# Weight loads one per batch, the table cleared at the start, turned maxima copied by ScalarE, and a new order for the end of the kernel

## What is computed

```python
# x: 16 batches x 128 rows x 512; ctx has the same shape; 8 heads, 8 experts
x = x + tanh(g_xattn) * xattn(layernorm(x), ctx, ctx)
x = x + tanh(g_ffn) * ffn(layernorm(x), wg, W, b)

# xattn: per head softmax(q^T k / 4) over 512 keys, times v
# ffn: a switch layer. each of the 2048 rows goes to one expert
idx  = argmax(softmax(xt @ wg))
gate = softmax(xt @ wg)[idx]
out  = gate * (W[idx] @ xt + b[idx])
```

## Time and profile before

| | us |
|---|---|
| median of three runs | 562.26 |
| the three runs | 562.48, 562.26, 553.67 |
| the profiled execution | 557.37 |
| its span, first to last instruction | 555.6 |
| busy in the span: PE / DVE / ACT / POOL | 498.3 / 436.1 / 349.5 / 343.9 |

### The profile page before, as it was taken

One profiled execution on the slowest core, in us unless ns is written; L12 is line 12 of the kernel. 1 busy time (PEld: TensorE's weight loads), 2 busy tenths in 40 slices (PEclk: granted clock), 3 DMA queues, 4 the chain that ended last, 5 costly groups with the idle time before them and its releaser, 6 DMA issues.

```text
span 555.6 us, 10053 instructions
## 1 busy us (share of the span) xinstructions
PE 498.3 (90%) x2539; PEld 177.6 (32%) x2580; DVE 436.1 (78%) x851; ACT 349.5 (63%) x428; POOL 343.9 (62%) x531
## 2 busy tenths in 40 slices
PE   0389999899999999999999999978899879899993
PEld 0012223232333333233333333322233134345441
DVE  5898989798898999989999989949788768334341
ACT  3226877778888888888887887945768831111110
POOL 7544476667676767777676787854275445645541
PEclk9999999999999999999999999979999999999998
DMA  4873546665565747565565847564669944643410
GB/s 137 240 160 119 145 119 202 176 181 171 159 168 163 199 126 228 162 182 166 163 196 127 235 130 199 184 162 102 175 187 309 334 176 159 208 148 107 126 59 0
DMA packets 51760, 92.96 MB, mean 167 GB/s; under 512 B 22898, under 2 KB 24946, under 8 KB 51688
## 3 DMA queue, kind: packets, MB, share of 16 engines
q1 hardware_dynamic: 36624, 67.33, 42.6%
q0 software_dynamic: 10560, 24.93, 13.9%
q10 hardware_dynamic: 4536, 0.23, 0.6%
HBM read 68.96 MB, written 28.41 MB: 175 GB/s over the span
## 4 chain that ended last, share of the span: by engine, by line
PE 62%; DVE 15%; DMA 10%; issue 4%; SPq 2%; ACT 2%; POOL 2%; ACTq 2%; POOLq 0%; DVEq 0%; another core or an unknown queue 0%
PE ps_pv L1382 17%; PE ps_ring L1340 17%; PE ps_scores L1359 14%; PE ps_scores L1443 10%; DVE neg_max L951 4%; DVE neg_max L1196 3%; DMA sums<-high_num 2%; DMA slot_tokens<-table_dram,slot_block 2%; DMA stacks<-shift_parts 2%; ACTq L842 2%; DMA sums<-low_num 1%; PE ps_scores L1426 1%; PE ps_ring L1345 1%; PE ps_ring L1402 1%; DMA recs<-recs_dram,token_cols 1%
## 5 line engine op out<-in xcount | busy, mean ns | idle before, releaser
L951 DVE TENSOR_REDUCE neg_max<-ps_ring 128x1 f32<-128x512 f32 x480 | 306.9, 681 | 29.0 <-PE ps_ring L1340 28.2
L852 ACT ACTIVATE probs<-ps_scores 128x1024 f32<-128x1024 f32 x256 | 251.6, 1023 | 65.9 <-PE ps_scores L1359 59.8
L1340 PE MATMUL ps_ring<-stacks 96*128 96x512 bf16 x480 | 166.9, 386 | 7.9 <-DVE neg_max L951 6.4
L1359 PE MATMUL ps_scores<-stacks 128*128 128x512 bf16 x471 | 145.4, 384 | 8.3 <-DMA stacks<-shift_parts 3.5
L1382 PE MATMUL ps_pv<-probs,v_ones 128*32 128x512 f32 x992 | 133.0, 608 | 0.1
L1340 PEld LDWEIGHTS ps_ring<-stacks 96*128 96x128 bf16 x480 | 46.6, 97 | 158.4 <-DVE neg_max L951 113.1
L1443 PE MATMUL ps_scores<-w_sb,f_xt 128*128 x184 | 83.5, 595 | 1.2 <-issue 1.2
L1359 PEld LDWEIGHTS ps_scores<-stacks 128*128 128x128 bf16 x512 | 48.2, 100 | 58.7 <-ACT probs L852 15.0
L828 ACT COPY f_xt<-ps_scores 128x512 f32<-128x512 f32 x22 | 12.9, 586 | 74.0 <-PE ps_scores L1426 74.0
L680 POOL DMA_INDIRECT recs<-recs_dram,token_cols x23 | 23.7, 1029 | 33.3 <-DVE y_outs L1164 16.0
L1443 PEld LDWEIGHTS ps_scores<-w_sb,f_xt 128*128 128x128 f32 x184 | 33.1, 190 | 34.6 <-issue 34.6
(11 more groups left out here) (144 smaller groups left out, 492.9 us busy)
## 6 DMA issues: line engine op xcount, KB each, us to landing
stacks<-parts_dram SPq DMA_DIRECT2D x224, 64.0 KB, 3.1
parts_dram<-prep POOLq DMA_DIRECT2D x15, 768.0 KB, 4.7
recs_dram<-rec SPq DMA_DIRECT2D x16, 512.0 KB, 3.7
w_sb<-w_t SPq DMA_DIRECT2D x16, 512.0 KB, 6.9
stacks<-parts_dram SPq DMA_DIRECT2D x32, 192.0 KB, 3.3
prep<-x_perm SPq DMA_DIRECT2D x16, 256.0 KB, 2.7
prep<-k_perm SPq DMA_DIRECT2D x16, 256.0 KB, 3.0
v_in<-v_t SPq DMA_DIRECT2D x16, 256.0 KB, 2.8
```

Source lines behind the costliest of these rows:

```text
L852: nc.scalar.activation(probs[:, k % 2, 2 * jp:2 * jp + 2], ps_scores[:, jp], ACT.Exp).then_inc(exp_done, 1)
L951: nc.vector.tensor_reduce(neg_max[:, g, j, c:c + 1], ps_ring[:, SLOT[tile]], AX.X, ALU.max, negate=True).then_inc(ring_free, 1)
L1340: nc.tensor.matmul(ps_ring[:, SLOT[tile]], q_stack[0:KS, into.p, g, j, c * 128:(c + 1) * 128], k_stack[0:KS, into.p, g, j], start=True, st ...
L1359: last = nc.tensor.matmul(ps_scores[:, jp, j % 2], k_stack[0:KA, B.p, g, j, c * 128:(c + 1) * 128], q_stack[0:KA, B.p, g, j], start=True, ...
```

## The change

The weights are loaded one piece per batch: piece 0 before batch 0, piece B in batch B, between the store and the spread of the high reciprocals. The table is cleared before batch 0. The two turned maxima of a batch get semaphores of their own (`turned_full`, `turned_taken`), so the ring counts 32 entries, and ScalarE copies them: the high half after the exponentials of step 0 and before `read_high`, the next batch's low half after those of step 4 and before `read_low`. Only the very first copy stays with VectorE.

At the end, `turn_slot(0)` moves behind the last values, and the routing of batch 14 behind it; only slot 0 is turned before the first expert, every next slot is turned in the middle of an expert. VectorE turns the last sums when the values are done, without waiting for ScalarE's read, and ScalarE's read waits for the turning. VectorE's `name_experts(1)`, `take_tiles(1)` and `take_columns(1)` come later, slot 0's bias earlier, and the counting of tiles of the last phase moves behind slot 2's combine. GpSimd reads the table for the second phase after the last norm's scale, and scatters before it waits for new columns.

```diff
-RING_FIRST, RING_BATCH = 1, 34
+RING_BATCH = 32
...
-NUMBER = {name: n for n, name in enumerate(e for e in ENTRIES if e not in ("rows", "route"))}
+NUMBER = {name: n for n, name in enumerate(e for e in ENTRIES if e[0] == "t" and e[:4] != "turn")}
...
+def turned(B, g):
+    return B.b * 2 + (g + 1)
...
+        turned_full, turned_taken = sem("turned_full"), sem("turned_taken")
...
+            def load_weight(B):
 
                 n = NC * NE * DM // NB
-                for piece in range(first, first + pieces):
-                    sp.dma_start(w_sb[:].rearrange("p c e n -> p (c e n)")[:, piece * n:(piece + 1) * n], w_t[piece]
-                                 ).then_inc(w_loaded, 16)
+                sp.dma_start(w_sb[:].rearrange("p c e n -> p (c e n)")[:, bass.ds(B.b * n, n)],
+                             w_t[bass.ds(B.b, 1)].rearrange("o p n -> (o p) n")).then_inc(w_loaded, 16)
+
+            def clear_table():
+
+                sp.wait_ge(pool_const, POOL_CONSTS)
+                sp.dma_start(table_dram.rearrange("(k h p) o -> k h (p o)", h=WIDE // 2, p=256 // WIDE),
+                             none_i[:].unsqueeze(1).to_broadcast([128, WIDE // 2, 256])).then_inc(table_set, 16)
...
+            clear_table()
+            load_weight(Batch(0, 0))
...
                 if prev and by_transfer(B.plus(-1)):
                     store_recips(B.plus(-1), 1)
+                    load_weight(B)
                     spread_recips(B.plus(-1), 1)
+                elif B.known(NB - 1):
+                    load_weight(B)
                 if prev and nxt:
                     load_values(B.plus(1))
-                if B.known(NB - 4):
-                    load_weights(0, 2)
-                if B.known(NB - 3):
-                    load_weights(2, 2)
-                if B.known(NB - 2):
-                    load_weights(6, 4)
-                if B.known(NB - 1):
-                    load_weights(10, 6)
...
-                if B.known(NB - 3):
-                    load_weights(4, 2)
...
-                if B.known(1):
-                    sp.wait_ge(pool_const, POOL_CONSTS)
-                    sp.dma_start(table_dram.rearrange("(k h p) o -> k h (p o)", h=WIDE // 2, p=256 // WIDE),
-                                 none_i[:].unsqueeze(1).to_broadcast([128, WIDE // 2, 256])).then_inc(table_set, 16)
...
-                if g == 1:
-                    pool.wait_ge(ring_free, ring_base(B) + (1 if B.known(NB - 1) else NUMBER["turn1"] + 1))
-                else:
-                    pool.wait_ge(ring_free, RING_FIRST if B.known(0) else ring_base(B.plus(-1)) + (NUMBER["turn0"] + 1))
+                pool.wait_ge(turned_taken, turned(B, g))
...
-                read_slots(1)
...
             rstd2(last)
+            read_slots(1)
             for s in range(NSLOT):
+                first = s + NREC in (PHASES[1][1], FIRST_LATE)
                 if s == 2:
                     number_places(3)
                     store_tokens(*GROUPS[3])
+                if first:
+                    scatter(s)
...
-                    wait(pool, y_ready, s + 1)
                     gather(s + NREC)
+                if not first:
+                    scatter(s)
                 if s == 2:
                     read_slots(2)
-                scatter(s)
...
+                if B.known(NB - 1):
+                    act.wait_ge(high_turned, NB - TURNED)
...
+            def take_maxima(B, g):
+
+                act.wait_ge(turned_full, turned(B, g))
+                stand_alone(act)
+                wait(act, shift_in[g], B.b * 48)
+                if not isinstance(B.b, int):
+                    stand_alone(act)
+                nc.scalar.copy(shift[:, g], ps_ring[0:NJ * NC, SLOT[("turn0", "turn1")[g]], 0:128]).then_inc(turned_taken, 1)
...
+                    if k == 0:
+                        take_maxima(B, 1)
                     if k == 0 and prev:
                         read_high(B.plus(-1))
+                    if k == NC and nxt:
+                        take_maxima(B.plus(1), 0)
...
+                if s == 2:
+                    norm2(Batch(7, 1))
                 if s == 3:
-                    norm2(Batch(7, 1))
                     take_rows(Batch(7, 1))
-                if s == 4:
                     exp_gates(3)
                 evacuate(s, turned_bank(s))
...
-            def take_maxima(B, entry, g, slot):
-
-                dve.wait_ge(ring_full, entry)
-                wait(dve, shift_in[g], B.b * 48)
-                nc.vector.tensor_copy(shift[:, g], ps_ring[0:NJ * NC, slot, 0:128]).then_inc(ring_free, 1)
+            def take_first_maxima():
+
+                dve.wait_ge(turned_full, 1)
+                nc.vector.tensor_copy(shift[:, 0], ps_ring[0:NJ * NC, 0, 0:128]).then_inc(turned_taken, 1)
...
-                dve.wait_ge((low_read, high_read)[g], B.b + 1)
+                if B.known(NB - 1) and g == 1:
+                    dve.wait_ge(pv_done, NB * STEPS)
+                else:
+                    dve.wait_ge((low_read, high_read)[g], B.b + 1)
...
-                take_maxima(B, ring_base(B) + 1, 1, SLOT["turn1"])
...
-                name_experts(1)
-                take_tiles(1)
...
-                        if at == (0, 2):
-                            take_maxima(B, base + (NUMBER["turn1"] + 1), 1, SLOT["turn1"])
-                        if at == (NC, 2):
-                            take_maxima(B.plus(1), base + (NUMBER["turn0"] + 1), 0, SLOT["turn0"])
...
             turn_sums(last, 1)
             invert_sums(last, 1)
+            add_bias(0)
+            take_logits(last.plus(-1))
             turn_back(last)
             add_attention(last)
-            take_logits(last.plus(-1))
-            take_columns(1)
-            add_bias(0)
             for s in range(NSLOT):
                 if s == 2:
                     take_logits(last)
                     find_experts(3)
                     find_gates(3)
+                    take_columns(1)
                     take_ranks(3, ps_ring[:, 0, RANK_AT:])
                     find_places(3)
+                    add_bias(2)
+                if s == 3:
                     count_tiles(2)
                     find_blocks(2)
-                if s == 3:
                     name_experts(2)
                 if s == 4:
                     take_columns(2)
                 combine(s, ps_y[:, s % 2])
-                if s + 1 < NSLOT:
+                if s + 1 < NSLOT and s != 1:
                     add_bias(s + 1)
+                if s == 0:
+                    name_experts(1)
+                    take_tiles(1)
...
+                elif held == "turn1":
+                    wait(pe, turned_taken, turned(B.plus(-1) if ago else B, 1))
+                elif held == "turn0":
+                    wait(pe, turned_taken, turned(B if ago else B.plus(1), 0))
...
-                    if k == 7 and B.known(NB - 1):
-                        pe.wait_ge(ranks_taken, 3)
-                        turn_slot(0, turned_bank(0))
...
+            pe.wait_ge(ranks_taken, 3)
+            turn_slot(0, turned_bank(0))
+            route(last.plus(-1))
             pe.wait_ge(w_loaded, 16 * NB)
-            turn_slot(1, turned_bank(1))
 
             def turn_next(s):
 
-                wait(pe, f_xt_ready, s)
-                turn_slot(s + 1, turned_bank(s + 1))
+                if s + 1 < NSLOT:
+                    wait(pe, f_xt_ready, s)
+                    turn_slot(s + 1, turned_bank(s + 1))
+
+            def rank_and_turn(s):
+                rank(3, ps_ring[:, 0, RANK_AT:])
+                turn_next(s)
 
             for s in range(NSLOT):
                 if s == 1:
-                    route(last.plus(-1))
-                if 0 < s and s + 1 < NSLOT and s + 1 != FIRST_LATE:
-                    turn_next(s)
-                if s == 2:
+                    expert(s, {2: lambda: turn_next(1), 3: lambda: turn_rows(last)})
+                elif s == 2:
                     route(last)
-                if s == 1:
-                    expert(s, lambda: turn_rows(last), 3)
-                elif s == 2:
-                    expert(s, lambda: rank(3, ps_ring[:, 0, RANK_AT:]))
-                elif s + 1 == FIRST_LATE:
-                    expert(s, lambda: turn_next(FIRST_LATE - 1))
+                    expert(s, {2: lambda: rank_and_turn(2)})
                 else:
-                    expert(s)
+                    expert(s, {2: lambda: turn_next(s)})
```

19 lines of the change are left out of this document (9 added, 10 removed).

## The result

| | before | after |
|---|---|---|
| median, 20 runs each | 559.56 | 549.87 |
| lowest to highest | 553.67 to 564.23 | 545.32 to 555.34 |
| ratio after to before | | 0.9827, interval 0.9803 to 0.9852 |
| profiled execution, its span | 557.37, 555.6 | 547.24, 545.6 |

The change gains 1.7%, about 9.7 us. The forecast of 540 had a gain of 19.7 by its sum, so half of it is missing.

What follows compares the result with a forecast made beforehand. The prediction took TensorE to set the pace in the middle; its terms summed to a gain of 19.7, giving 537.7 from the profiled 557.37 or 542.6 from the median 562.26; it said 540, range 531 to 550.

Steps and rivals of the forecast that it cites:

- rival 1: Tail gives nothing because another late gather replaces the one removed; gain 12.9, time 547; chance 0.14.
- Rival 2: Stalls of batches 12 to 14 come from stack loads and the store, half of 10.1 stays; 545; chance 0.09.
- What bounds the kernel: In the middle TensorE sets the pace; VectorE and ScalarE cost time only where TensorE waits for them.
- Table clearing: Moving it from the end of batch 1 to the start gains 2.8 in batch 2 and costs 0.5 at the start.
- three pieces in a row at the quickest landing, less some 7: Upper bound on the start's loss: 9.6 less some 7 between SP's issue and ScalarE's cast for batch 3, 2.6.
- ScalarE idle for parts in batch 0 for more than 1 us: Sign, at the start of the loop, that would show the forecast wrong.
- Weights: One piece per batch gains 5.2, 4.3 and 0.6 in batches 12, 13 and 14, and costs 0 in the loop.
- Rival 3: Weights delay the spread by 1.0 us in each of 13 batches, giving back 13; 553; chance 0.11.
- Rival 4: Weight piece ahead of the spreads in SP's queue delays them, deciding at 5.4 landing; up to 574, slower; chance 0.04.
- Maxima by ScalarE: Copies moved from VectorE gain 0.5 in batches 9 to 11, 13 and 14, price 0 in the body.
- Batch 15 to the first expert: Turning of slot 0 0.6, shorter shift-row wait 0.7, copy wait -0.3, earlier first expert 1.8; gain 2.8.
- The first eight slots: TensorE's work of 33.4 less 0.95, plus 1.5 idle, makes 34.0 of 38.04; gain 4.0.

Runs made afterwards that it cites:

- u_double: Changed kernel, table clearing and first weight piece issued after batch 2's parts landed, plus a second, unread 512 KB piece in batches 1 to 13; 553.62 us.
- u_endw: Changed kernel, but weights loaded as before in batches 12 to 15, none in the loop; 558.51 us, ratio 0.9965 to the kernel before.
- b_weights: Kernel before, with only the weights loaded one piece per batch, the first once the parts of batch 2 had landed; 548.51 us, ratio 0.9803.
- u_read: Changed kernel, but GpSimd issues the third table read ahead of the scatter of slot 2; 545.18 us, ratio 0.9776 to the kernel before.
- u_turn: Changed kernel, but the record of slot 7 is turned behind the whole of expert 6, not in its middle; 548.45 us, ratio 0.9791.
- after_again: The changed kernel itself, unedited, run once more beside other variants on one chip; 549.20 us, ratio 0.9824 to the kernel before.
- u_onehot: Changed kernel, but in batch 13 VectorE finds experts five maxima later and ScalarE takes their exponentials one step later; 546.57 us, ratio 0.9760.
- x_plain: Changed kernel with weights loaded late as before, VectorE copying the maxima, and the table cleared once batch 2's parts had landed; 554.18 us, ratio 0.9896.
- u_clear: Changed kernel, but table clearing and first weight piece are issued only when the parts of batch 2 have landed; 545.61 us, ratio 0.9781.
- u_vcopy: Changed kernel, but VectorE copies the turned maxima as before, with the new semaphores kept; 548.47 us, ratio 0.9818 to the kernel before.
- the three best versions: Changed kernel with later clearing, one-hot, slot 7 turning and first bias, and earlier third table read; 539.79 and 541.90 us, or 539.56 with VectorE copying maxima.

## Why the prediction was wrong, step by step

The forecast added up to 19.7, and the parts below to 8.5 in means of the stretches. The largest pieces of the difference are 3.8 in the tail (5.8 forecast, 2.0 measured), 3.0 at the start (a loss of 0.5 forecast, 3.5 measured) and 2.6 in batches 12 to 14. That the time, 549.87, still lies just under the upper end of the range, 550, was luck: that end was set for rivals 1 and 2, and the loss at the start is in neither.

**What bounds the kernel.** Right. TensorE's busy time did not move, and every gain and loss is one of its waits, but for what the lower clock costs in the tail.

**Table clearing.** The gain in batch 2 was right (2.8 forecast; 24.41 to 26.23 in the kernels with it moved, 25.2 in their mean, u_double aside, against 27.29 and 27.90 in the two with the old place: 2.4). The price at the start failed: 0.5 taken, 2.6 as upper bound, 3.5 measured in the mean of six. The step that failed is "three pieces in a row at the quickest landing, less some 7". It set the landing times of the new transfers against empty DMA engines. In the kernel before, the engines were 0.77 and 0.87 busy in 42 to 46 already, and the store landed at 47.35. 1.5 MB more, at some 320 GB/s by the windows above, are an estimated 4.9 of work; the store landed 5.1 to 6.1 later than before, counted from its issue, and 2.8 later with 1 MB (an estimated 3.3). And what the cast's lateness is worth was not asked: 1.1 late cost nothing (u_endw), 3.2 to 4.8 late cost 2.1 to 4.6. The mechanism was named with its place and its indicator ("ScalarE idle for parts in batch 0 for more than 1 us"); only the size was off.

**Weights.** The mechanism was right, the largest term was too large: 10.1 for batches 12 to 14, 7.5 measured in means. Of the 2.6 missing, 1.3 are the one-hot in batch 13. The forecast compared it with batch 9, which does the same finding of experts; but in batch 13 the one-hot meets GpSimd's 128x512 multiplication or addition and in batch 9 it does not. The row was in the trace of before: 0.94 us for an instruction that takes 0.19 elsewhere, with TensorE waiting 1.15 behind it. The rest is one profile: batch 12 took 29.98 in the profile of before and 27.20 to 28.56 in three others with late weights. The price of 0 in the loop holds as far as can be seen. Rival 2 is out: with late weights and all else changed (u_endw) the stalls of batches 12 to 14 are back. Rival 3, 1.0 a batch, is out too. Rival 4's mechanism, a piece that delays the spreads behind it, came out in u_double only; one piece landed in 3.6 in the median, as this row of b_weights (tile w_sb) says, and in 3.5 to 3.7 in the six other profiles with one piece a batch that have a landing time, well under the 5.4 at which rival 4 was to decide:

```profile
DMA to landing us min/median/max: 3.1/3.6/8.8
```

**Maxima by ScalarE.** 0.5 was forecast, none is seen (rival 5). The copy takes 0.24 to 0.26, a little under the 0.27 it was valued at and the 0.29 of the estimate.

**Batch 15 to the first expert.** Right. From the turning of batch 15 to the last values 1.1 less (1.0 forecast; but b_weights, with the old tail, takes 19.6 here too, so most of it is the weights', and the 0.6 for the turning of slot 0 is not shown), last values to first expert 1.91 against 3.46 (1.6 forecast; 1.35 in most of the other runs).

**The first eight slots.** The step that failed most: 38.0 was to become 34.0 and became 39.3. The forecast filled the slots with TensorE's work, 33.4, and left 1.5 for idle time, naming the chain from the last record to the record of slot 7 but not measuring it. That chain can be read from the end of the last values to the turning of slot 7: 448.07 to 481.05 before, 32.98; 438.39 to 471.73 after, 33.34, the longest of the eight kernels with this tail and neither mend (31.45 to 32.35 in the seven others; 32.50 and 32.15 in the two others with the old tail). It is what bounds the slots, and starting the experts 1.5 earlier only makes TensorE wait longer for it, 2.87 instead of 0.48. Up to the table writes the change shortens the chain (first write 19.3 after the last values before, 17.6 after, 16.1 to 17.0 in those seven); the scatter put ahead of the table read gives most of that back (u_read), and turning slot 7 in the middle of expert 6 keeps half an expert waiting with it (u_turn). This is rival 1, "another late gather takes the place of the one removed", to which 0.14 had been given, and with it the time is 547. In the first pair of profiles the tail gives 0.3, in the means below 2.0, so that rival is nearer than the forecast's 5.8 (1.8 and 4.0), but not all of it.

**The clock.** Close to the end of the wait for slot 7 (0.3 ahead of it in after, 0.6 to 1.0 behind it in the others) the granted clock fell to 0.50, which is 1.2 GHz, for 3.4 us, in after, after_again, u_endw, u_onehot, x_plain and u_double (and once in the old tail, in b_weights, whose slots took 41.3, 2.1 behind a wait of 1.29 that followed one of 1.56); the windows of u_clear and u_vcopy show 1.00 throughout, with the same order of the tail. In the first six TensorE had been idle 2.38 to 2.87 there. In u_read, u_turn and the three best versions, with waits of 1.59 and less at that place, it never fell in the slots. The eight slots take 38.1 to 39.3 with the fall and 36.7 and 36.9 without: 2.0. The forecast had no term for it. Windows of the changed kernel around that wait, then of u_clear (idle 2.52 ahead of 469.39); the third column from the right is the clock:

```profile
469.00:471.00 2.00, 0.00 (x0) 0.00 (x0) 0.00 (x0) 0.00 (x0) 1.67 (x2) 1.00 0.83 252
471.00:473.00 2.00, 1.27 (x5) 1.25 (x6) 0.00 (x0) 0.14 (x1) 1.42 (x2) 0.61 0.76 201
473.00:475.00 2.00, 2.00 (x3) 0.67 (x2) 0.00 (x0) 0.44 (x1) 0.61 (x1) 0.54 0.97 305
```

```profile
469.00:471.00 2.00, 1.60 (x7) 1.07 (x8) 0.00 (x0) 0.59 (x1) 1.40 (x2) 1.00 0.81 246
471.00:473.00 2.00, 2.00 (x6) 0.89 (x5) 1.13 (x2) 0.00 (x0) 0.63 (x1) 1.00 0.95 264
```

**The sum again**, in means of the stretches: table -3.5 + 2.4, weights 7.5 and 1.4 in batch 15, batches 3 to 8 -1.3 (scatter or copies), tail 41.7 in the three kernels with the old one against 39.7 in the eight with the new one and neither mend: 2.0. Together some 8.5, of 9.7 measured.

**What stays open.** Why batches 3 to 8 take 148.0 to 151.7 in most of the others and 146.8 to 147.8 in four kernels in which VectorE copies. It is not the weights alone: u_endw has none in the loop and is the slowest. TensorE's stalls there are of 0.4 to 1.1 us each, two to four in a slow batch, and in the three slowest, u_double aside, more than half of the excess is in batches 3 and 4 (27.72 for batch 3 in after_again, 24.72 before); no run tried a cause. Why the clock fell in six of the eight profiles with this tail and neither mend, and not in the other two, was not tried either.

## What to carry to other kernels

Price a transfer that is moved into a new stretch against the bytes already on the DMA engines there and against the slack of the first reader behind it, not against its own landing time; the free place was 6 us further on in the same trace. Before filling a stretch with the busiest engine's work, measure the dependent chain that runs through it from end to end, across all engines, and look for what an edit puts into that chain. And when a batch is priced by its sister, compare the durations of the small instructions too.
